# A mixture feed-forward in which the video expert's late tokens of two examples share one product

## The reference, cut to what matters

```python
def expert_mask(tt):                       # tt is 1 for the padded tokens at an example's end
    vm = jnp.zeros(tt.shape, dtype=bool)
    return vm.at[:, :-1].set((tt[:, :-1] == 1) & (tt[:, 1:] == 1))
...
mi = rms_norm(hidden_states, ln_post_attn_w)                 # 8 x 256 tokens of 256
v_out = jax.nn.silu(mi @ v_gate) * (mi @ v_up) @ v_down      # 256 -> 688 -> 256
l_out = jax.nn.silu(mi @ l_gate) * (mi @ l_up) @ l_down
hidden_states = hidden_states + jnp.where(vm, v_out, l_out)
```

## Time and profile before

| | |
|---|---|
| median of 3 runs | 1439.62 us (1439.02 to 1447.79) |
| the profiled execution, its own time | 1439.24 us |
| its span, from the first to the last instruction | 1437.5 us |
| TensorE matmuls | busy 1383.1 us, 96% of the span |
| VectorE, ScalarE, GpSimd | 791.9, 501.0 and 349.7 us |

### The profile page before, as it was taken

The page is one execution under the profiler, slowest core; times in us unless marked ns, Lnnn a source line. Parts: engine busy times, 40 slices in busy tenths (PEclk is TensorE's granted clock), DMA queues, the critical chain, the costliest instruction groups (busy, mean ns, idle before and its releaser), DMA issues.

```text
span 1437.5 us, 27076 instructions
## 1 busy us (share of the span) xinstructions
PE 1383.1 (96%) x11507; PEld 1116.1 (78%) x11507; DVE 791.9 (55%) x1490; ACT 501.0 (35%) x845; POOL 349.7 (24%) x382
## 2 busy tenths in 40 slices
PE   7988799999999999999999999999899999999998
PEld 5866578787787788888888888776678788787776
DVE  4555686766666665443333433245676665756653
ACT  3333332423423322244434544333341332423321
POOL 1243342222323120111011111224332323222210
PEclk9998999999999999999999999989999999999999
DMA  9010000000010001200000000011000000000000
GB/s 317 2 59 1 2 2 2 1 1 2 1 45 2 2 23 34 98 1 0 1 0 1 0 1 1 1 40 41 2 2 9 2 9 9 2 8 5 6 8 16
DMA packets 19906, 27.36 MB, mean 19 GB/s; under 512 B 3432, under 2 KB 15552, under 8 KB 19520
## 3 DMA queue, kind: packets, MB, share of 16 engines
q1 hardware_dynamic: 19008, 24.20, 5.1%
q10 hardware_dynamic: 768, 1.26, 0.3%
HBM read 23.35 MB, written 2.10 MB: 18 GB/s over the span
## 4 chain that ended last, share of the span: by engine, by line
PE 90%; DVE 4%; ACT 2%; issue 1%; POOL 1%; DMA 0%; SPq 0%; POOLq 0%; ACTq 0%; DVEq 0%
PE bank L1234 15%; PE bank L1259 8%; PE bank L1122 6%; PE bank L975 5%; PE bank L1458 4%; PE row_banks L1105 4%; PE bank L1465 4%; PE row_banks L1365 4%; PE bank L1422 4%; PE row_banks L1072 4%; PE bank L1040 3%; PE bank L968 3%; PE row_banks L1077 2%; PE row_banks L1394 2%; PE row_banks L1319 2%; PE bank L1201 2%
## 5 line engine op out<-in xcount | busy, mean ns | idle before, releaser
L1606 ACT ACTIVATE room<-bank 128x256 f32<-128x256 f32 x176 | 66.8, 383 | 218.4 <-PE bank L1234 169.3
L1811 DVE TENSOR_REDUCE room<-row_banks 128x4 f32<-128x512 f32 (+1 forms) x128 | 116.7, 954 | 46.7 <-PE row_banks L1077 46.5
L1234 PE MATMUL bank<-room,gate_w 128*128 128x256 f32 (+1 forms) x640 | 135.9, 335 | 5.1 <-DVE room L1898 2.2
L1895 DVE SCALAR_TENSOR_TENSOR room<-room,bank 128x256 f32<-128x256 f32 x176 | 73.3, 417 | 107.1 <-ACT room L1606 106.9
L1234 PE MATMUL bank<-room,up_w 128*128 128x256 f32 (+1 forms) x640 | 130.9, 327 | 0.0
L1576 ACT ACTIVATE room<-row_banks 128x1536 f32<-128x1536 f32 x64 | 92.9, 1452 | 102.7 <-PE row_banks L1105 102.7
L1259 PE MATMUL bank<-room,down_w 128*128 128x256 f32 (+1 forms) x704 | 128.5, 332 | 0.0
L840 POOL TENSOR_SCALAR_AFFINE_SELECT room<-room 128x1024 f32<-128x1024 f32 x64 | 71.1, 1110 | 216.7 <-ACT room L1576 216.7
L1234 PEld LDWEIGHTS bank<-room,gate_w 128*128 128x128 f32 x640 | 98.5, 190 | 32.2 <-issue 18.0
L1259 PEld LDWEIGHTS bank<-room,down_w 128*128 128x128 f32 x704 | 109.8, 191 | 9.9 <-issue 0.7
L1234 PEld LDWEIGHTS bank<-room,up_w 128*128 128x128 f32 x640 | 103.0, 191 | 8.3
(11 more groups left out here) (228 smaller groups left out, 2642.1 us busy)
## 6 DMA issues: line engine op xcount, KB each, us to landing
out_x<-wq SPq DMA_DIRECT2D x8, 256.0 KB, 2.2
qkv<-in_L_xattn_v_qkv SPq DMA_DIRECT2D x2, 768.0 KB, 6.1
qkv<-in_L_xattn_l_qkv SPq DMA_DIRECT2D x2, 768.0 KB, 8.9
gate_w<-in_L_xattn_v_gate SPq DMA_DIRECT2D x2, 640.0 KB, 8.8
gate_w<-in_L_xattn_l_gate SPq DMA_DIRECT2D x2, 640.0 KB, 7.6
up_w<-in_L_xattn_v_up SPq DMA_DIRECT2D x2, 640.0 KB, 6.3
up_w<-in_L_xattn_l_up SPq DMA_DIRECT2D x2, 640.0 KB, 6.5
down_w<-in_L_xattn_v_down SPq DMA_DIRECT2D x2, 640.0 KB, 6.5
```

Of the source, the lines that this page charges most:

```text
L1234: last = pe.matmul(b[:, j * S + lo:j * S + hi], w[:, k, f * P:(f + 1) * P], y[:, k, lo:hi], start=(k == 0), stop=(k == KT - 1))
L1811: last = dve.tensor_reduce(dst, row_banks[:, :, P * i:P + S * i], X, ALU.max, negate=True)
```

## The change

The video expert's 64 late columns leave the tile loop. The parts are:

- `up(e, i)` now has six tiles, five language tiles and the shared rest. The early video columns (the 192 inside the branch) are added into the language tile's own bank, so that the branch now stands between the first and the second half of the gate product and again of the up product.
- `late_y` (GpSimd) copies the 64 late columns of `ff_yv` of two examples side by side into `ff_late`, 128 columns.
- `late_up`, `late_tanh`, `late_hidden` and `late_down` do the five video tiles once for a pair of examples, with 128 columns, in three groups of two, two and one tile; they run with the second example of each pair. `late_give` adds the result to both examples, in two operations.
- Since early video tokens now share the hidden tile of the language expert, GpSimd parts them with the mask (`by_expert`): two operations of 192 columns for each of the five tiles of each example, done whether there are such tokens or not. `down(e, i)` waits for them.
- Output: the rows of an example are turned once the pair is done, with two row buffers in place of one.
- The table of times that sets the order is new throughout, for all layers.

The sum of the work for TensorE in the built programs: 6121 matmuls are run before and 5881 after (branches not taken left out). Of those with 128x128 weights, 784 have 64 columns before and 304 after; 574 have 128 columns before and 814 after. All other shapes are equal in number. The branches are 224 before and 304 after, and the number of places where the array's tile shape changes from one matmul to the next is 537 before and 515 after.

The diff, cut to its core (the table of times is left out but for a line of each side):

```diff
-FF_ORDER = [f for i in range(FULL) for f in (FULL + i, i)] + [2 * FULL]
+UPS = FULL + 1
+LATE_TILES = [(0, 1), (2, 3), (4,)]
...
-FEED_STARTS = [[540.881, 614.859, 684.882, 752.036, 813.837, 871.887, 943.790, 1004.643],
+FEED_STARTS = [[1366.590, 1432.609, 1496.448, 1561.540, 1628.005, 1685.541, 1795.398, 1846.583],
...
+                def late_y(e):
+                    pool.wait_ge(*CRS_DVE.did(e, "yv"))
+                    if e >= 2:
+                        pool.wait_ge(*FF_PE.did(e // 2 * 2 - 1, "vup2"))
+                    pool.tensor_copy(ff_late[:, :, e % 2, :], ff_yv[:, :, LATE:]).then_inc(*FF_POOL.does(e, "late"))
+
+                def by_expert(e, i):
+                    pool.wait_ge(*FF_DVE.did(e, f"hid{i}"))
+                    pool.tensor_tensor(hid_v[:, i, :], hid[:, i, 0:LATE], seen(e)[:, 0:LATE], ALU.mult)\
+                        .then_inc(*FF_POOL.does(e, f"hv{i}"))
+                    pool.wait_ge(*FF_POOL.did(e, f"hv{i}"))
+                    pool.tensor_tensor(hid[:, i, 0:LATE], hid[:, i, 0:LATE], hid_v[:, i, :], ALU.subtract)\
+                        .then_inc(*FF_POOL.does(e, f"hl{i}"))
...
                 def up(e, i):
-                    f = FF_ORDER[i]
+                    f = FULL + i
...
-                    if f < FULL:
-                        with pe.If(has_early[e % B]):
-                            columns(ff_yv, 0, LATE)
-                        last = columns(ff_yv, LATE, S)
-                    elif f < 2 * FULL:
-                        last = columns(ff_yl, 0, S)
-                    else:
-                        for m, w in enumerate((gate_w, up_w)):
+                    for m, w in enumerate((gate_w, up_w)):
+                        if f < 2 * FULL:
+                            out = b[:, m * S:(m + 1) * S]
+                            pe.matmul(out, w[:, 0, f * P:(f + 1) * P], ff_yl[:, 0, :], start=True, stop=False, skip_group_check=True)
+                            with pe.If(has_early[e % B]):
+                                for k in range(KT):
+                                    pe.matmul(out[:, 0:LATE], w[:, k, i * P:(i + 1) * P], ff_yv[:, k, 0:LATE],
+                                              start=False, stop=False, skip_group_check=True)
+                            last = pe.matmul(out, w[:, 1, f * P:(f + 1) * P], ff_yl[:, 1, :], start=False, stop=True, skip_group_check=True)
...
+                def late_up(e, g):
+                    if g == 0:
+                        pe.wait_ge(*FF_POOL.did(e - 1, "late"))
+                        pe.wait_ge(*FF_POOL.did(e, "late"))
+                    pe.wait_ge(*FF_DVE.did(e, ("hid4", "hid5", "vhid0")[g]))
+                    b = ff_bank[(g + 1) % 2]
+                    for j, f in enumerate(LATE_TILES[g]):
+                        for m, w in enumerate((gate_w, up_w)):
+                            for k in range(KT):
+                                at = (2 * j + m) * P
+                                last = pe.matmul(b[:, at:at + P], w[:, k, f * P:(f + 1) * P],
+                                                 ff_late[:, k].rearrange("p e n -> p (e n)"), start=(k == 0), stop=(k == KT - 1))
+                    last.then_inc(*FF_PE.does(e, f"vup{g}"))
...
                 def down(e, i):
-                    f = FF_ORDER[i]
-                    pe.wait_ge(*FF_DVE.did(e, f"hid{max(i, NF - 2)}"))
+                    f = FULL + i
+                    if i == 0:
+                        pe.wait_ge(*FF_DVE.did(e, "vhid1" if e % 2 else "hid5"))
+                    pe.wait_ge(*(FF_POOL.did(e, f"hl{i}") if i < FULL else FF_DVE.did(e, f"hid{i}")))
...
+                def late_down(e, g):
+                    pe.wait_ge(*FF_DVE.did(e, "vhid2"))
+                    for f in LATE_TILES[g]:
                         for t in range(KT):
+                            last = pe.matmul(ff_bank[1][:, t * P:(t + 1) * P], down_w[:, f, t * P:(t + 1) * P], hid_late[:, f, :],
+                                             start=(f == t == 0), stop=(f == FULL - 1), skip_group_check=True)
+                    last.then_inc(*FF_PE.does(e, f"vdown{g}"))
...
                 def turn_out(e):
-                    pe.wait_ge(*FF_DVE.did(e, "x4"))
+                    pe.wait_ge(*FF_DVE.did(e | 1, "xv"))
...
+                def late_give(e):
+                    dve.wait_ge(*FF_PE.did(e, "vdown2"))
+                    dve.wait_ge(*FF_DVE.did(e, "x4"))
+                    for k, done in ((0, "xv0"), (1, "xv")):
+                        x, late = late_of(e, k), ff_bank[1][:, k * P:(k + 1) * P].rearrange("p (e s) -> p e s", e=2)
+                        dve.scalar_tensor_tensor(x, late, 0.5, x, ALU.mult, ALU.add).then_inc(*FF_DVE.does(e, done))
```

More of the change, by code:

```diff
@@ L172, in put @@
         at.append((time, stage, *which))
-    put(-20549.8448, "x_out")
-    put(-1254.5657, "x_turn")
+    put(-26058.4378, "x_out")
+    put(1926.6632, "x_turn")
     return at
@@ L370, in feed_stages @@
[L370 to L385 removed]
+    put(-1071.2339, "by_expert", 0)
@@ L560, in whole_order @@
         each(CROSS_STARTS[layer], cross_stages(), layer * B)
-        each(FEED_STARTS[layer], feed_stages(layer == 1), layer * B)
+        each(FEED_STARTS[layer], feed_stages(), layer * B)
+        order.extend((LATE_STARTS[layer][e // 2] + time, stage, layer * B + e, *which) for e in range(1, B, 2)
+                     for time, stage, *which in late_stages())
+    each(FINAL_STARTS, final_stages(), B)
     each(GATED_STARTS, gated_stages())
```

704 lines of the change are left out of this document (372 added, 332 removed).

## The result

The changed kernel takes 1429.73 us (median of 6 runs, 1427.79 to 1435.82), the kernel before 1439.32 us beside it (6 runs): ratio 0.9928, 95% interval 0.9910 to 0.9946. That is 10 us faster, where 56 were forecast. The profiled execution took 1428.92 us with a span of 1427.0.

The account below looks back on a forecast made before the run. TensorE's work, busy 1383.1 of 1437.5 us, was taken to bound the kernel, with 54.4 us standing. Terms summed to -56.6 from 1439.24, giving 1382.6 and a median of 1383.0 us; range 1366 to 1402.

Parts of the forecast that it names:

- the fillings: Starts of second and fourth layers: q, k and v of the next example cover one wait each, -3 us twice.
- the two last examples: Cross-attention of examples 7 and 15, at layer ends: little cover left between steps, +2.5 and +4.2 us.
- the tail: End of the kernel, from 1403 us: stalls at up tiles go, some waits are added, in all -3.5 us.
- the pair's waits: Up and down products waiting for the pair's hidden values: 8 pairs x 0.25 us, +2 us.
- 22.6 us "elsewhere": Part of TensorE's 54.4 us idle in the kernel before, outside the three named stretches, which have 31.8.
- Products and shapes: Video tiles on TensorE: 480 fewer instructions at 112 ns, -53.8 us; 22 fewer tile-shape changes, -2.0 us.
- Rival 3: Pair's products: 128 columns cost twice what 64 cost, nothing of the 53.8 us left, 1436.8 us; chance 0.02.
- Branches: 304 instead of 224, the examples' 240 amid language tiles: covered by the product before, 0 us, bounds 0 and 27.
- rival 4: The examples' 240 branches stop TensorE, each exposing 207 to 342 ns: slower, up to 1465 us; chance 0.02.
- Rival 1: GpSimd's selects hold up the masking by 1 to 2 us in each of 16 passes: 1399 to 1415 us; chance 0.11.
- Rival 2: The new table, in all layers, closes more of TensorE's idle time than counted: about 1362 us; chance 0.08.

Follow-up runs that it names:

- e1: Changed kernel with only the pairing undone, each 128-column product of the pair made as two of 64 columns: 1488.71 us, ratio 1.0342 to the kernel before.
- e5: Changed kernel without the 240 branches of the up and down products and their bodies: 1432.48 us, ratio 0.9936 to the kernel before.
- e2: Changed kernel without GpSimd's parting of the hidden tiles (by_expert, 160 operations): 1442.44 us, ratio 0.9979 to the kernel before.
- e12: The kernel of e9 without GpSimd's parting of the hidden tiles: 1385.16 us, ratio 0.9616 to the kernel before.
- e6: Changed kernel's work in a second searched order, with table loads above all taken into account: 1388.63 us, ratio 0.9611 to the kernel before.
- e9: Changed kernel's work in a third searched order, concentrated TensorE holes counted dearer than spread ones: 1388.17 us, ratio 0.9641 to the kernel before.
- e3: Changed kernel's operations and waits in a first searched order of the same stages on each engine: 1406.03 us, ratio 0.9770 to the kernel before.
- e8: Changed kernel with only the first layer and the second layer's first two examples in another order: 1425.81 us, ratio 0.9877 to the kernel before.
- e11: Changed kernel with example 14's last up tile moved on TensorE between cross_values and cross_project of example 15: 1433.49 us, one run.
- e13: Changed kernel with VectorE's cross-value copies moved ahead of the previous example's four products, in three places: 1431.25 us, ratio 0.9934 to the kernel before.
- e14: Changed kernel with GpSimd's four two-input turning operations replaced by one-input multiplications by zero: 1436.6 us, one run.

## Why the prediction was wrong

**The step that failed** is the overlap. The holes were taken from the old order's trace and carried over to the new order, but for six small terms: -3 and -3 for the fillings, +2.5 and +4.2 for the two last examples, -3.5 for the tail, +2 for the pair's waits, together -0.8 us. Measured are +30.4 us of holes and +14.1 of lower clock. The work itself came off nearly as counted, so the pricing of the products was right and the forecast that no new holes would stand beside it was wrong.

**What bounds the kernel.** Right for the kernel before: PE's busy time in the steady parts. The conclusion drawn from it, that what PE is spared "comes off in full", holds for the old order only, and the change replaces that order. The clock was misread too: it is not 1.00 outside the two fillings but 0.94 from 1000 to 1100 us, with 7.1 us of holes there, part of the 22.6 us "elsewhere" that the prediction never looked into.

**Products and shapes.** Forecast -55.8, measured -55.0 of work at the full clock. That the two agree so closely is in part luck: e1 prices the pairing at 49.7 in the same order, the pairs of searched orders have 46.7 to 49.0 between them, and the work of the kernel before comes out at 1348 to 1361 us depending on its order. Steps are 112 ns at 64 and 128 columns, as taken from the earlier trace rows. Rival 3 falls. The -2.0 for the changes of shape is too small to be told apart by any run here.

**Branches.** Taken as 0, measured 1.8 us, no more than the scatter (e5); rival 4 falls.

**GpSimd.** Forecast 433 us of busy time, measured 446.8: the operations take 0.59 and 0.55 us, not 0.48, so the straight line from 512 and 256 columns was too low at 192. It holds nothing up in the changed kernel (e2), and 3 us at most where holes are few (e12). Rival 1 falls.

**Examples 7 and 15 and the tail.** The places were right. In example 7 PE waits 2.24 us ahead of the sums (527.80 us) and 1.04 ahead of the spread, where it waited 0.46 before: 2.8 us for the 2.5 forecast. In example 15 it is 1.80 us ahead of the sums, 2.34 ahead of `cross_project`, no wait for hidden values at any up tile, 0.49 ahead of `down` 0 for the 0.7 forecast:

```profile
1368.90 0.61 PE L1048 MATMUL bank<-mean_w,room 128*128 128x1 f32 x4 [1.80 <-POOL room L852]
...
1389.88 1.13 PE L1270 MATMUL bank<-room,cd_w 128*128 128x256 f32 x4 [2.34 <-DVE room L1964]
...
1414.04 5.45 PE L1329 MATMUL bank<-room,down_w 128*128 128x256 f32 x24 [0.49 <-DVE room L1998]
```

From 1300 to 1403 us the holes are 6.5 us more, where 4.2 were forecast. The tail gave 2.3 us for the 3.5 forecast. The pair's own waits, forecast at 2 us, are 1.4.

**The fillings.** Forecast -3 twice; this term had the wrong sign. Up to 200 us PE's holes are 8.4 us more than before (29.5 to 37.9) and the clock's loss about 10 more; the fourth layer's filling is 0.9 us better in its holes and the 100 us behind it 3.1 worse. I read one exchange in the table (q, k and v ahead of the row maximum) as one wait covered. In the fourth layer the like wait (2.56 us at 1008.30) is gone. In the second it stands as it did, ahead of the same second scores:

```profile
163.53 1.66 PE L1166 MATMUL row_banks<-room 32*128 32x256 f32 x16 [2.54 <-DVE room L1903]
```

And I didn't look at what else had moved: the first projections of the second layer now start at about 85 us, after the whole fusion, and did at about 65 while the fusion still ran.

**The steady parts.** No term was given to them but the pair's waits, and between 200 and 550 us there are 12.6 us of holes more (2.8 of them example 7's), with 6.5 of clock. They are many small ones, 1.53 us at first scores, 0.2 at the second scores, 0.24 at `cross_first`, in every pass or every second one, and two at `dense` of 3.49 and 1.90 us. The largest is a coincidence of two engines' operations that the old trace doesn't have at this place. It has one such product elsewhere, 1.49 us at 939.0 us beside GpSimd's line 834.

**The clock.** The forecast gave it 0.5 us at example 15 and "a little" in the fillings; it cost 14.1 us. Its loss was 40% of the holes before (21.6 of 54.4) and 42% after (35.7 of 84.8), a ratio that the old trace had to offer. Over the other runs it is 28 to 70%, so it is a size and no law.

**Rival 2** was the right question with the wrong sign: the new table is new everywhere, and it opens 30 us of holes more than it closes. A rival "the new table is worse" had no place among mine. e6 shows that the order, and not the pairing, is where the missing 47 us can be had: the same work in another order takes 1388.6 us, 5.6 over the forecast. That this lands so near is no merit of the forecast, which was made for the table as it stands.

What stays open: how much of e6's and e9's lower clock could be had back, since e9 didn't lower its loss of 33.3 us, and e3, with 22.4, had 69.4 us of holes; and the share of each move of the table, of which only e8's, e11's and e13's were tried apart: e8's gave 6 us up to the end of the second layer, the other two nothing.

## What to carry to other kernels

Here 32-bit weights with 64 columns of work behind them cost what 128 cost; sharing them between two examples halves the cost, and that was worth 47 to 50 us of work in every order, though only 28 to 40 us of time between the pairs of searched orders. But where a change brings a new order of the whole program, the order is a term of its own, of either sign and as large as the gain: give it a row in the sum and a rival on either side, and price it by holes and by the clock behind them, which in the 16 profiled executions here took another 28 to 70% of the holes. Test order and work apart (the old work in a new order, the new work in another) before believing either, and read holes and clock from the trace, since runs of one kernel can lie 17 us apart with the clock (e2: 1427.6 us at 0.975, 1445.1 at 0.961).

## What the hardware showed that I had not expected

- VectorE's scalar_tensor_tensor with two inputs in SBUF (128x256) takes 0.48 us alone, 1.28 to 1.36 us beside GpSimd's operations with two inputs, and 0.50 us in the mean of four beside its operations with one (e14; 0.48 three times, 0.83 once). In the changed kernel that made the largest hole, 3.49 us.
- ScalarE's change between gelu and exp costs a table load of 1.28 us each time. An order that alternates them makes 33 loads where one that groups them makes 17. Whether PE pays for it hangs on the order: with 35 loads PE had no hole in the third layer of the kernel before, with 33 in e3 one of 2.38 us.
- The clock doesn't fall behind large holes alone: in e2 PE ran 13.7 us at the lower level behind holes of 0.8 and 0.25 us, and in the changed kernel, with the same order and the same holes at this place, none. Why is not shown. e2's ten times lie in two clusters, at 1428 to 1433 and at 1441 to 1445 us; e13's ten spread evenly from 1428 to 1439.
